# Scales of the feed-forward tiles on GpSimd instead of VectorE, the gate's Tanh over its input, a column of scales per tile, new call lists and banks

## The chip, the cores and the metric

The kernel runs on one core of one Trainium2 chip. Its five instruction queues are those of TensorE (PE), VectorE (DVE), ScalarE (ACT), GpSimd (POOL) and SyncE (SP); each works strictly in order and they meet only at semaphores. The metric is the device time of one execution in microseconds (us), median over several runs; less is better.

## The reference

One layer over x of shape (4, 256, 256): a two-way linear recurrence feeds a gated state-space block, and a second one feeds a quantised feed-forward block. Cut to what matters:

```python
# recurrence, used twice with other w and u (k = v = fside)
ek = exp(min(k, 30)); ekv = ek * v
nf, df = scan(a*decay + ekv), scan(b*decay + ek)        # forward over time, and the same backward
r = sigmoid(x) * (nf + nb - ekv + euk*v) / max(df + db - ek + euk, 1e-8) * (0.8 + 0.2*tf)
# attention
z, xc, B, C, dt = split(r @ in_proj_w); xc = silu(causal_conv1d(xc))
y = ssd_chunked(elu(C)+1, elu(B)+1, xc, exp(-dt*exp(A_log))) + D*xc
x = x + (rms_norm(y) * norm_scale * silu(z)) @ out_proj_w
# feed-forward, on h = second recurrence gated with x
def act_quant(x):  s = 127 / clip(max|x|, 1e-5);  return clip(round(x*s), -128, 127) / s
h = silu(act_quant(rms_norm(h)) @ weight_quant(w1).T + b1)
h = layer_norm(gelu(h)) * ln_g + ln_b
x = x + act_quant(rms_norm(h)) @ weight_quant(w2).T + b2
```

## The kernel before

The batch index b has four values. For each b the kernel does: the recurrences of both blocks at once on DVE (four forward scans, L1230; four backward, L1239; `add_own`, L1250; a reciprocal by one Newton step from a seed that ACT makes with Relu, Ln, Exp, `recip`; `ratio`; `gated`, L1277, which makes uT); the attention block on PE, ACT and DVE (`features`, `conv_in`, `gate_in`, DVE's `conv_taps` L1323, `conv_turns`, `running_sums`, `log_decays`, ACT's `decays` L844, DVE's `attend` L1347, `within`, `between`, `y_turns`, `project`); and the feed-forward block. That one works in eight tiles i of 128 rows, two for each b. `PARTS` numbers five parts p: for b = 0, 1, 2 both tiles together, and the last two tiles, 6 and 7, alone as p = 3 and 4.

A part's steps are `residual` (DVE L1375), `gate_h` (ACT), `ffn_in` (DVE), `square_h` (ACT), `norm_h` (POOL), `ffn_in_max` and `ffn_in_scale` (DVE, hm and its reciprocal hq), `quantise_h` (POOL L542), `q1_turns` (PE), `turned_q1` (ACT L888). A tile's steps are `ffn_diag` (POOL L482), `ffn_up` (PE; four matmuls of the activations with w1T and then four records of the bias row with the tile's diagonal, b1b and diag), `ffn_silu`, `ffn_gate` (tiles 4 to 7), `ffn_gelu`, `ffn_mean`, `ffn_var` (ACT L918), `ffn_dev` (POOL), `ffn_center` and `ffn_shift` (DVE L1435, L1443), `ffn_square` (ACT L930), `ffn_rms` (POOL), `ffn_max` and `ffn_scale` (DVE), `ffn_round` (POOL L576), a turn of the rounded tile (a DMA transpose for tiles 0 to 5, PE and ACT for 6 and 7), `ffn_down` (PE), `ffn_out` (DVE L1472) and `store` (SP).

Small scales go with it. `ffn_in_back` on DVE makes al1, which takes the product back to real units, two columns per part, and its reciprocal ral1, with which `ffn_diag` scales the identity, so that the bias is right before al1 is applied. `ffn_back` on DVE makes al2 for `ffn_out`. The scales of a part (hss, hmv, hr, hmx, hfl, hm, hq) live in tiles of two columns that the next part writes again, so `norm_h`, `ffn_in_max`, `ffn_in_scale` and `square_h` wait for the last readers of the part before. `gate_x` (ACT L752) writes Tanh of xcT into one buffer th, and so waits for `gated` of the b before.

The order of all this is written by hand at the end of each engine's block, as one list of calls; that list is the schedule. `HOME` gives every product its PSUM bank, and the bare `pe.wait_ge` lines between PE's calls wait until a bank's last reader is done. `warm(k)` issues eight matmuls that nobody reads. SP's list is the order of the loads, of `spread_sums` (six small DMAs that carry cum_s to cum_t, needed by `log_decays`), of the transposes `turn_q2` and of the stores. ACT's list also names its table loads.

Of the kernel before, what the change touches and what calls it, by code (L numbers as in the profile page):

```python
# [15 lines left out]
P = 128  # L16
# [14 lines left out]
    "warm": (4, 2, 1, 3, 5, 0, 4, 1, 2, 6),  # L31
    "cond_sum": 1,
    "weight_sums": 7,
    "features": (7, 1, 6, 5),
    "conv_in": ((3, 2), (6, 3), (4, 1), (6, 0)),
    "conv_turns": ((2, 3), (7, 2), (1, 0), (7, 6)),
    "gate_in": ((5, 1), (3, 5), (6, 4), (4, 5)),
    "r2_turns": (0, 4, 7, 7),
    "scores": (6, 0, 5, 4),
    "log_decays": (((0, 0), (5, 2)), ((6, 3), (5, 7)), ((6, 0), (0, 4)), ((7, 5), (2, 3))),  # L40
    "running_sums": (4, 1, 2, 5),
    "within": ((0, 2), (3, 5), (1, 4), (5, 6)),
    "between": (5, 2, 0, 2),
    "y_turns": ((5, 2), (1, 0), (2, 7), (2, 3)),
    "project": (1, 1, 0, 7, 6),
    "q1_turns": (0, 3, 3, 2, 2),
    "ffn_up": (2, 6, 2, 0, 4, 0, 6, 2),
    "weight_columns": 1,
    "ffn_turns": ((0, 0), (0, 0), (0, 0), (0, 0), (0, 0), (0, 0), (6, 7), (2, 3)),
    "ffn_down": (7, 3, 4, 5, 0, 1, 4, 5),  # L50
# [3 lines left out]
def build(nc, x, xT, kT, condT, wcol, prm, hprm, in_w, out_w, w1, w2, b1, ln_g, ln_b, b2, out):  # L54
# [23 lines left out]
    with ExitStack() as ctx:  # L78
# [15 lines left out]
        PARTS = [(b, 0, TT) for b in range(B - 1)] + [(B - 1, c, c + 1) for c in range(TT)]  # L94

# [66 lines left out]
        th = sb("th", [P, CT * T])  # L162
# [47 lines left out]
        ral1 = sb("ral1", [P, NT])  # L210
# [90 lines left out]
        def _(sp):  # L301
# [94 lines left out]
            store(4)
            store(5)
# [6 lines left out]
        def _(pool):  # L404
# [1666 lines left out]
```

## Time and profile before

| | us |
|---|---|
| median of 3 runs | 205.26 (204.13 to 205.44) |
| span of the profiled execution | 201.1 |
| TensorE busy in it | 159.6 |
| VectorE busy in it | 178.6 |
| ScalarE busy in it | 159.8 |
| GpSimd busy in it | 100.3 |

The span runs from the first to the last instruction of one execution; what the run's time has over it lies outside (before the first and behind the last instruction). Starts in the rows are microseconds from the span's start. A float32 matmul stands in the rows as two records of PE, so "x16" of float32 is eight matmuls, and the lengths given for single records overlap: a stretch is best read from start to start.

### The profile page before, as it was taken

To read this page: it belongs to the slowest core of one execution; us is meant where nothing else is said; L and a number is where in the kernel's file an instruction comes from. 1 tells how busy PE (TensorE), PEld (TensorE's weight loads), DVE (VectorE), ACT (ScalarE), POOL (GpSimd) and SP (SyncE) were. 2 spreads that over 40 slices of the span, in tenths; PEclk is the share of its full clock that TensorE was granted. 3 is DMA by queue.
4 is the path that set the end of the run, shared out by engine and by line. 5 is a ranking of instruction groups with operands and counts; after the bars stand their busy time and mean duration, and the time that the engine had idled before them with its cause. 6 is when DMAs were issued, how large, how long until landed. Compare 5 with 4: busy or idle time off the path is not lost.

```text
span 201.1 us, 3190 instructions
## 1 busy us (share of the span) xinstructions
PE 159.6 (79%) x903; PEld 117.4 (58%) x908; DVE 178.6 (89%) x320; ACT 159.8 (79%) x293; POOL 100.3 (50%) x172
## 2 busy tenths in 40 slices
PE   7800039459799999999999999999999999672844
PEld 5600038334589867698757488957668766350633
DVE  2899999999999999899999899979866769998991
ACT  5860599969699279998789999899999886877632
POOL 3609759000426523758700086467455287858570
PEclk9975557958999999999999999999999999999699
DMA  4999603200000000000000000000240000602312
GB/s 133 320 385 382 248 2 104 106 3 2 1 0 3 0 0 2 4 3 0 2 2 3 0 0 3 0 2 0 54 96 14 0 0 0 130 7 49 81 60 96
DMA packets 12304, 11.55 MB, mean 57 GB/s; under 512 B 7680, under 2 KB 10368, under 8 KB 12032
## 3 DMA queue, kind: packets, MB, share of 16 engines
q1 hardware_dynamic: 11856, 11.33, 18.1%
q8 instruction: 7, 0.11, 0.2%
q14 instruction: 9, 0.07, 0.1%
q10 hardware_dynamic: 432, 0.03, 0.1%
HBM read 8.69 MB, written 1.05 MB: 48 GB/s over the span
## 4 chain that ended last, share of the span: by engine, by line
PE 45%; DVE 14%; ACT 12%; issue 12%; POOL 8%; DMA 5%; SPq 3%; POOLq 1%; DVEq 0%; ACTq 0%
PE banks L1688 41%; DVE Ys L1239 5%; DMA wn<-wn 4%; PE banks L1685 3%; DVE Fs L1230 3%; DVE nd L1250 3%; SPq L355 2%; ACT Ys L744 1%; POOL qr L514 1%; ACT Ys L742 1%; POOL wn L576 1%; ACT dec L691 1%; ACT dec L844 1%; ACT D L724 1%; DMA cum_t<-cum_s 1%
## 5 line engine op out<-in xcount | busy, mean ns | idle before, releaser
L1688 PE MATMUL banks<-inw,uT 128*128 128x8 f32 (+1 forms) x64 | 21.7, 465 | 19.4 <-DVE uT L1277 19.4
L1688 PEld LDWEIGHTS banks<-inw,uT 128*128 128x128 f32 x64 | 10.9, 217 | 24.7 <-issue 24.5
L1230 DVE TENSOR_TENSOR_SCAN Fs<-D,E 128x514 f32<-128x514 f32 x16 | 23.0, 1460 | 0.5 <-POOL D L449 0.5
L1688 PE MATMUL banks<-uT,inw 128*128 128x256 f32 x80 | 20.3, 398 | 0.0
L1239 DVE TENSOR_TENSOR_SCAN Ys<-D,Fs 128x514 f32<-128x514 f32 x16 | 19.7, 1250 | 0.0
L1323 DVE SCALAR_TENSOR_TENSOR cv<-banks,cols,cv 128x255 f32<-128x255 f32 (+2 forms) x48 | 19.4, 472 | 0.1
L1688 PEld LDWEIGHTS banks<-uT,inw 128*128 128x128 f32 x80 | 15.2, 197 | 4.2 <-issue 2.1
L508 POOL TENSOR_TENSOR vs<-vv,grow 128x512 f32<-128x512 f32 x4 | 4.5, 1121 | 25.8 <-issue 20.3
L1688 PEld LDWEIGHTS banks<-vv,skips 128*128 128x128 f32 x128 | 15.2, 192 | 1.9 <-issue 1.8
L495 POOL TENSOR_TENSOR own<-own,vT 128x1024 f32<-128x1024 f32 x4 | 12.1, 3025 | 8.4 <-DVE own L1220 8.4
L1688 PE MATMUL banks<-vv,dec 128*128 128x64 f32 x128 | 15.6, 275 | 0.0
L1688 PE MATMUL banks<-vv,skips 128*128 128x64 f32 x128 | 15.3, 273 | 0.0
L1688 PE MATMUL banks<-b1b,diag 128*128 128x512 f32 x32 | 15.0, 592 | 0.0
L1688 PE MATMUL banks<-outw,yzT 128*128 128x256 f32 x64 | 15.0, 382 | 0.1
L1688 PEld LDWEIGHTS banks<-vv,dec 128*128 128x128 f32 x128 | 14.9, 192 | 0.0
L501 POOL TENSOR_TENSOR nd<-nd,Ys 128x512 f32<-128x512 f32 x4 | 5.2, 1301 | 17.5 <-DVE Ys L1261 17.5
L1688 PE MATMUL banks<-w2T,wn 128*128 128x256 f16 x64 | 9.0, 290 | 6.0 <-DMA wn<-wn 6.0
L1688 PE MATMUL banks<-starts 128*128 128x256 bf16 x80 | 12.1, 317 | 1.3 <-POOL starts L429 1.3
L1688 PEld LDWEIGHTS banks<-outw,yzT 128*128 128x128 f32 x64 | 11.8, 190 | 2.3 <-issue 0.5
L742 ACT ACTIVATE Ys<-nd 128x1024 f32<-128x1024 f32 (+1 forms) x5 | 4.4, 885 | 9.9 <-DVE nd L1250 9.9
L930 ACT ACTIVATE wn<-wn,grs 128x1024 f16<-128x1024 f32 x8 | 9.2, 1146 | 2.6 <-DVE wn L1443 1.5
L1347 DVE TENSOR_TENSOR dec<-dec,banks 128x1024 f32<-128x1024 f32 x8 | 9.7, 1210 | 1.7 <-ACT dec L844 1.7
(205 smaller groups left out, 469.4 us busy)
## 6 DMA issues: line engine op xcount, KB each, us to landing
wn<-in_w_dram SPq DMA_DIRECT2D x2, 1024.0 KB, 11.1
inw<-in_in_w_dram SPq DMA_DIRECT2D x1, 1160.0 KB, 10.8
vT<-in_kT_dram SPq DMA_DIRECT2D x4, 256.0 KB, 8.2
xcT<-in_xT_dram SPq DMA_DIRECT2D x4, 256.0 KB, 9.6
xn<-in_x_dram SPq DMA_DIRECT2D x4, 256.0 KB, 6.0
out_dram<-ot SPq DMA_DIRECT2D x8, 128.0 KB, 1.7
outw<-in_out_w_dram SPq DMA_DIRECT2D x1, 512.0 KB, 5.7
b1b<-in_b_dram SPq DMA_DIRECT2D x1, 512.0 KB, 8.6
```

The source lines that it names most:

```text
L495: pool.tensor_tensor(own[:, b % 2, :, 1, :], own_e(b), vT[:, b].unsqueeze(1).broadcast_to([P, 2, CT * T]), ALU.mult)\
L501: pool.tensor_tensor(nd[:, 1, 1], nd[:, 1, 1], rn[:, 1], ALU.mult).then_inc(rat2_ok, 1)
L508: pool.tensor_tensor(by_head(vs[:]), by_head(vv[:, b % 2, 0]), grow[:, 0, :].unsqueeze(2).broadcast_to([P, NH, HD]), ALU.mult).then_inc(vs ...
L742: act.activation(seed, den, ACT.Relu, bias=-DEN_FLOOR).then_inc(rl_ok, 1)
L930: act.activation(Q2[:, i % 2], Y[:, i % 2], ACT.Square, scale=grs[:, i:i + 1], accum_out=qss[:, i:i + 1])\
L1230: dve.tensor_tensor_scan(Fs[:, w, k], D[:, w, 0:CT * TS], E[:, b % 2, k].rearrange("p c t -> p (c t)"), 0.0, ALU.mult, ALU.add).then_inc(f ...
L1239: dve.tensor_tensor_scan(Ys[:, w, k][:, ::-1], D[:, w, 1:CT * TS + 1][:, ::-1], Fs[:, w, k][:, ::-1], 0.0, ALU.mult, ALU.add).then_inc(ys_ ...
L1250: last = dve.scalar_tensor_tensor(nd[:, :, w, s], y, gap[:, w, ct, b:b + 1], own[:, b % 2, w, :, s], ALU.mult, ALU.add)
L1323: dve.scalar_tensor_tensor(cv[:, ft, back:], at("conv_in", b, i)[:, j * T:(j + 1) * T - back], cols[:, w:w + 1], cv[:, ft, back:], ALU.mul ...
L1347: dve.tensor_tensor(dec[:, c], dec[:, c], at("scores", b)[:, c * P:(c + 1) * P].unsqueeze(1).broadcast_to([P, NH, P]), ALU.mult).then_inc( ...
L1685: return pe.transpose(dst, src, ident[0:n, 0:n])
L1688: return pe.matmul(dst, lhsT, rhs, start=start, stop=stop)
```

## The change

`ffn_in_back` and `ffn_back` are gone from DVE. POOL's `ffn_diag` makes al1 and a second column hsw (the root of the mean square over the weight scale), and the diagonal from hsw and hq; `ffn_round` makes al2 behind the rounding. The scales have one column per tile, and the waits for their last readers are gone. `gate_x` writes over xcT. Every call list is new, and so are the banks in `HOME` and the bare waits that go with them.

```diff
             def ffn_diag(i):
+                s = slice(i, i + 1)
                 pool.wait_ge(ident_ok, 2)
-                pool.wait_ge(al1_ok, 2 * part_of(i) + 2)
+                pool.wait_ge(hr_ok, part_of(i) + 1)
+                pool.wait_ge(hq_ok, part_of(i) + 1)
+                pool.wait_ge(wmean_ok, 3)
+                pool.tensor_scalar(al1[:, s], hm[:, s], hr[:, s], (wmean if i < FIRST_TANH else whalf)[:, 0:1], ALU.mult,
+                                   ALU.mult).then_inc(al1_ok, 1)
+                pool.tensor_scalar(hsw[:, s], hmv[:, s], hr[:, s], wrec[:, 0:1], ALU.mult, ALU.mult).then_inc(al1_ok, 1)
                 if i >= 2:
                     pool.wait_ge(h_ps, i - 1)
-                pool.tensor_scalar(diag[:, i % 2], ident[:], ral1[:, i:i + 1], 1.0 if i < FIRST_TANH else 0.5, ALU.mult, ALU.mult).then_inc(dg_ok, 1)
+                pool.wait_ge(al1_ok, 2 * i + 2)
+                pool.tensor_scalar(diag[:, i % 2], ident[:], hsw[:, s], hq[:, s], ALU.mult, ALU.mult).then_inc(dg_ok, 1)
...
                 pool.tensor_scalar(Q2[:, i % 2], Y[:, i % 2], qq[:, i:i + 1], ROUND16, ALU.mult, ALU.add)\
                     .then_inc(Q2_ok, 1)
+                s = slice(i, i + 1)
+                pool.wait_ge(qr_ok, 2 * (i + 1))
+                pool.tensor_scalar(al2[:, s], qm[:, s], gq[:, s], wmean[:, 1:2], ALU.mult, ALU.mult).then_inc(al2_ok, 1)
...
             def gate_x(b):
                 act.wait_ge(xT_in[b], 16)
-                if b >= 1:
-                    act.wait_ge(u_ok, b)
-                act.activation(th[:], xcT[:, b], ACT.Tanh, scale=0.5).then_inc(th_ok, 1)
+                act.activation(xcT[:, b], xcT[:, b], ACT.Tanh, scale=0.5).then_inc(th_ok, 1)
```

Of the lists, these parts matter most to the text below (the list after; "..." marks what is left out):

```text
SP    load_k(1) load_cond load_k(0) load_outw load_b1 load_xT(0) load_w1 load_xT(1) load_w2 ... load_inw ...
ACT   load_decw exp_w cond_tanh load_cols wkv_exp(0) wkv_exp(1) wkv_own(0) ...   (the first table load is no longer named)
PE    cond_sum warm(6) features(0) conv_in(0,1) conv_in(0,0) warm(8) ...          (before: 48 warm matmuls stood ahead of features(0))
DVE   ... ratio(0) forward(1,0,0) gated(0) recip(0,1,2) forward(1,0,1) forward(1,1,0) features(0) softplus_in(0)
      conv_taps(0,1) softplus_out(0) ... running_sums(0) wkv_min(2) conv_taps(0,0) recip(1,0,2) own_min(2) ratio(1) gated(1) forward(2,0,0) ...
DVE   ... recip(2,0,2) wkv_min(3) ratio(2) forward(3,0,0) gated(2) conv_taps(1,0) residual(0) ...
PE    ... project(0) log_decays(1,0,1) log_decays(1,1,0) features(2) gate_in(2,0) log_decays(1,1,1) conv_turns(1,0) conv_turns(1,1) ...
PE    ... within(3,0) q1_turns(2) r2_turns(3) between(3) ffn_up(4) y_turns(3,0) within(3,1) project(3) y_turns(3,1)
      weight_columns project(4) ffn_up(5) ffn_down(0) q1_turns(3) q1_turns(4) ffn_down(1) [wait Y_ok 5] ffn_up(6) ffn_up(7)
      [waits] ffn_down(2) ffn_down(3) ffn_down(4) ffn_down(5) ffn_turns(6,*) ffn_turns(7,*) ffn_down(6) ffn_down(7) [wait ot_ok 7] warm(0) warm(3)
ACT   ... turned_y(3,0) ffn_square(2) ffn_silu(4) ffn_square(3) square_y(3,1) ffn_gelu(4) turned_y(3,1) gate_h(3) weight_columns
      square_h(3) ffn_var(4) gate_h(4) square_h(4) ffn_silu(5) turned_q1(3) ffn_gelu(5) turned_q1(4) ffn_var(5) ffn_square(4)
      ffn_silu(6) ffn_square(5) ffn_gelu(6) ffn_silu(7) ffn_var(6) ffn_gelu(7) ffn_var(7) ffn_square(6) ffn_square(7) ...
DVE   ... ffn_shift(3) ffn_gate(4) ffn_scale(2) norm_gate(3,1) residual(3) ffn_max(3) ffn_mean(4) ffn_in(3) ffn_scale(3) residual(4)
      ffn_in_max(3) ffn_in(4) ffn_in_scale(3) ffn_in_max(4) ffn_center(4) ffn_in_scale(4) ffn_gate(5) ffn_shift(4) ...
```

Before, PE's list at this place was `within(3,0) between(3) q1_turns(2) within(3,1) y_turns(3,0) ffn_up(4) y_turns(3,1) project(3) ffn_up(5) project(4) q1_turns(3) ffn_down(0) ffn_down(1) [wait ot_ok 1] ffn_up(6) q1_turns(4) ffn_down(2) ffn_down(3) [wait ot_ok 2] ffn_up(7) ffn_down(4) warm(2) warm(7) ffn_down(5) ...`, with `weight_columns` far earlier and `r2_turns(3)` ahead of `within(3,0)`.

## Rows read from the trace of the kernel before

**Rows 1.** The page: busy tenths of each engine in 40 slices of the span
```profile
PE   7800039459799999999999999999999999672844
DVE  2899999999999999899999899979866769998991
ACT  5860599969699279998789999899999886877632
```

**Rows 2.** Windows: stretch, its length, busy us and instructions of each engine, PEclk, DMA
```profile
100.00:149.60 49.60, 49.10 (x258) 34.59 (x260) 44.60 (x78) 46.64 (x78) 21.20 (x38) 1.00 0.05 12
149.60:168.75 19.15, 19.10 (x115) 14.47 (x114) 14.01 (x29) 17.71 (x33) 10.86 (x30) 1.00 0.08 15
168.75:201.10 32.35, 18.65 (x124) 12.60 (x124) 26.39 (x49) 18.83 (x33) 20.60 (x47) 0.95 0.27 66
```

**Rows 3.** Groups by line, DVE: the scales that the change takes away
```profile
L1464 DVE TENSOR_SCALAR al<-qm,gq,wmean 128x1 f32<-128x1 f32 x8 | 2.0, 266 | 0.0
L1416 DVE TENSOR_SCALAR al<-hm,hr,whalf 128x1 f32<-128x1 f32 x4 | 1.0, 263 | 0.0
L1420 DVE RECIPROCAL ral<-al 128x2 f32<-128x2 f32 (+1 forms) x5 | 0.8, 165 | 0.2
```

**Rows 4.** Groups by line, POOL: its nearest operations to the added ones
```profile
L567 POOL TENSOR_SCALAR qfl<-qmv,qr,stdf 128x1 f32<-128x1 f32 x8 | 2.7, 334 | 0.0
L566 POOL TENSOR_SCALAR gq<-qr,grs 128x1 f32<-128x1 f32 x8 | 2.1, 264 | 0.8
L482 POOL TENSOR_SCALAR diag<-ident,ral 128x128 f32<-128x128 f32 x8 | 3.0, 371 | 8.0 <-issue 7.9
```

**Rows 5.** Timeline of the start: ACT's table load and Exp; then DVE's first scan
```profile
1.20 1.28 ACT L946 ACT_TABLE_LOAD   x1 [1.20 <-PEq L2061]
2.50 0.20 ACT L675 ACTIVATE ew<-decw 128x4 f32<-128x4 f32 x1
...
7.06 2.34 DVE L1230 TENSOR_TENSOR_SCAN Fs<-D,E 128x514 f32<-128x514 f32 x1 [0.53 <-POOL D L449]
```

**Rows 6.** Timeline: a scan beside a long product of POOL, and one alone
```profile
14.67 3.19 POOL L495 TENSOR_TENSOR own<-own,vT 128x1024 f32<-128x1024 f32 x1 [6.34 <-DVE own L1220]
15.64 3.30 DVE L1230 TENSOR_TENSOR_SCAN Fs<-D,E 128x514 f32<-128x514 f32 x1
54.03 1.22 DVE L1230 TENSOR_TENSOR_SCAN Fs<-D,E 128x514 f32<-128x514 f32 x1
```

**Rows 7.** Timeline: uT of b = 0, 1 and 2 on DVE, and the first cum_t on PE
```profile
26.84 1.56 DVE L1277 SCALAR_TENSOR_TENSOR uT<-th,nd 128x512 f32<-128x512 f32 x1
51.83 0.38 PE L1688 MATMUL banks<-cum_t,cum_s 99*128 99x512 bf16 x1 [1.38 <-DMA cum_t<-cum_s]
55.17 0.66 DVE L1277 SCALAR_TENSOR_TENSOR uT<-th,nd 128x512 f32<-128x512 f32 x1
82.99 0.68 DVE L1277 SCALAR_TENSOR_TENSOR uT<-th,nd 128x512 f32<-128x512 f32 x1
```

**Rows 8.** Timeline of the end: PE's anchor, project(4), quantise_h(4), ffn_up(7)'s bias, the last two roundings
```profile
151.53 1.95 PE L1688 MATMUL banks<-vv,dec 128*128 128x64 f32 x16
166.87 1.89 PE L1688 MATMUL banks<-outw,yzT 128*128 128x256 f32 x8
174.39 0.48 POOL L542 TENSOR_SCALAR h<-h,hq 128x256 f32<-128x256 f32 x1
180.35 1.88 PE L1688 MATMUL banks<-b1b,diag 128*128 128x512 f32 x4
...
193.30 2.33 POOL L576 TENSOR_SCALAR wn<-wn,qq 128x1024 f16<-128x1024 f32 x2
```

**Rows 9.** Windows of PE's clock: after the pause from 182.2, and the last stage
```profile
182.00:184.00 2.00, 0.34 (x2) 0.00 (x0) 1.45 (x5) 1.42 (x2) 1.82 (x4) 1.00 0.00 0
189.00:190.00 1.00, 1.00 (x6) 0.73 (x5) 0.94 (x1) 0.00 (x0) 0.85 (x3) 0.50 0.00 0
196.00:198.00 2.00, 2.00 (x23) 1.71 (x21) 0.48 (x1) 1.16 (x3) 0.44 (x1) 1.00 0.37 123
```

More of the change, by code:

```diff
@@ L30 @@
 HOME = {
[L31 to L50, printed above, removed]
+    "warm": (6, 7, 6, 0, 2, 1, 1, 6, 5, 7),
+    "cond_sum": 0,
+    "weight_sums": 1,
+    "features": (2, 0, 2, 3),
+    "conv_in": ((4, 3), (7, 3), (3, 7), (6, 7)),
+    "conv_turns": ((4, 4), (0, 6), (5, 3), (4, 4)),
+    "gate_in": ((0, 1), (0, 1), (3, 2), (5, 6)),
+    "r2_turns": (2, 4, 6, 4),
+    "scores": (5, 5, 0, 5),
+    "log_decays": (((3, 2), (6, 7)), ((4, 6), (4, 4)), ((7, 1), (5, 7)), ((1, 7), (6, 7))),
+    "running_sums": (3, 4, 1, 0),
+    "within": ((2, 6), (0, 1), (0, 7), (6, 6)),
+    "between": (1, 6, 3, 5),
+    "y_turns": ((0, 6), (4, 4), (1, 4), (7, 6)),
+    "project": (0, 2, 0, 7, 4),
+    "q1_turns": (2, 6, 7, 6, 5),
+    "ffn_up": (4, 1, 2, 0, 2, 0, 2, 5),
+    "weight_columns": 5,
+    "ffn_turns": (0, 0, 0, 0, 0, 0, (5, 2), (3, 2)),
+    "ffn_down": (7, 4, 0, 1, 7, 4, 6, 7),
 }
@@ L650, in _ @@
             ffn_rms(4)
+            residual_bias(3)
             ffn_rms(5)
@@ L1547, in _ @@
             conv_taps(1, 0)
-            recip(2, 0, 2)
-            ratio(2)
             residual(0)
-            wkv_min(3)
-            gated(2)
+            softplus_in(2)
+            attend(1, 0)
+            softplus_out(2)
+            forward(3, 0, 1)
+            forward(3, 1, 0)
             ffn_in(0)
-            attend(1, 0)
+            own_min(3)
             ffn_in_max(0)
-            forward(3, 0, 0)
-            forward(3, 0, 1)
+            features(2)
+            forward(3, 1, 1)
@@ L1558, in _ @@
+            attend(1, 1)
+            running_sums(2)
+            conv_taps(2, 1)
             y_scale(1)
[L1559 to L1560 removed]
+            clip_weights(0)
+            backward(3, 0, 0)
+            norm_gate(1, 0)
             ffn_in_scale(0)
[L1562 to L1569 removed]
@@ new lines, in _ @@
+            pe.wait_ge(r2_ok, 3)
+            conv_in(3, 0)
+            pe.wait_ge(ty_ok, 3)
+            features(3)
+            pe.wait_ge(att_ok, 6)
+            within(2, 0)
+            pe.wait_ge(cv0_ok, 7)
+            pe.wait_ge(tap_ok, 42)
+            within(2, 1)
+            pe.wait_ge(cv0_ok, 8)
+            pe.wait_ge(tap_ok, 48)
+            q1_turns(1)
+            pe.wait_ge(Y_ok, 1)
+            conv_turns(3, 0)
+            gate_in(3, 0)
+            pe.wait_ge(q1T_ok, 2)
+            gate_in(3, 1)
@@ L1992, in _ @@
-            r2_turns(3)
-            pe.wait_ge(dex_ok, 14)
+            pe.wait_ge(dex_ok, 15)
             within(3, 0)
-            pe.wait_ge(dex_ok, 15)
-            between(3)
             pe.wait_ge(dex_ok, 16)
             q1_turns(2)
+            pe.wait_ge(vv_ok, 8)
+            r2_turns(3)
+            pe.wait_ge(att_ok, 8)
+            between(3)
+            pe.wait_ge(Y_ok, 3)
+            ffn_up(4)
+            y_turns(3, 0)
             within(3, 1)
-            y_turns(3, 0)
-            ffn_up(4)
+            project(3)
```

785 lines of the change are left out of this document (365 added, 420 removed).

## The prediction

> **What bounds the kernel now.** I read the page's tenths first [rows 1]. DVE is full from the first scan (7 us) on, PE has almost nothing to do until about 28 us, and from about 60 us to 165 us PE is full too. The windows say it more exactly [rows 2]: from 100 to 149.6 us PE is busy 49.1 of 49.6 us, and to 168.75 us 19.1 of 19.15, while DVE has 5.0 and 5.1 us free there. ACT has 3.0 and 1.4 us free. Behind 168.75 us no engine is full (DVE 26.4 of 32.35 us, PE 18.7): there the last two tiles walk from engine to engine. So there are three stages. Up to uT of b = 1 (55.8 us [rows 7]) DVE's order sets the time. From there to about 165 us PE's queue does. The last 32 us are a chain of latencies, whose length the order on DVE, ACT and POOL decides. I take the stages apart in that order and ask of each what the new lists make of it, adding durations along the new lists.
>
> **The small scales.** DVE loses eight al2 of 0.266 us, eight al1 of 0.263 (two groups like the row) and five reciprocals of 0.165 [rows 3]: 2.1 + 2.1 + 0.8 = 5.0, by the rows' totals 4.7 us. Nearly all of it lies behind 90 us, where DVE had 5 us free in 50 anyway, so up to 168.75 us it is worth nothing; the cover is PE's full queue. POOL gains 24 operations. Each has three small operands, like qfl at 0.334 us, and the lower bound is gq with 0.264 [rows 4]. I take 0.33, as the operands are like qfl's, and 0.07 for each diagonal, which now multiplies by two columns: 24 x 0.33 + 8 x 0.07 = 8.5 us on an engine that has 38 of 68 us free between 100 and 168.75 us [rows 2]. Ahead of a diagonal al1 and hsw are 0.7 us, but PE asks for the diagonal only after q1_turns, ACT's copy and half of `ffn_up`, over 1 us later: nothing. The one place on the path is al2 of tile 6 between the last two roundings, 0.33 us.
>
> **Start, up to uT of b = 1.** Three things change. (a) The table load of 1.28 us is no longer named ahead of the first Exp [rows 5]. If it now runs behind the wait for decw it costs up to 1.28 us, if ahead of it nothing. Before, the load ran from 1.20 to 2.48 us and the Exp began at 2.50, so some of it stays covered: I take 0.5, bounds 0 and 1.28. The cond_sum no longer stands behind eight warm matmuls, but its load is now behind load_k(1): a wash. (b) `forward(1,0,0)` stands ahead of gated(0), and conv_taps(0,1) ahead of running_sums(0), while forward(2,0,0) now follows gated(1). Counting DVE's work between the first scan and gated(1), `forward(2,0,0)` goes out (-1.2), own_min(2) comes in (+0.6), and conv_taps(0,1) has to wait for PE and ACT at the half clock that follows 19 us of pause (about +1.3). (c) DVE's scans are held up by POOL's long products: the scan at 15.64 us took 3.30 us beside one and a scan alone 1.22, so 2.1 us were lost there [rows 6]. In the new order the first such product starts while five small operations stand between it and the next scan, so about 1 us less is lost. The sum is +0.5 - 1.2 + 0.6 + 1.3 - 1.0 = +0.2; I call it 0, with bounds -1.2 and +1.3. The first cum_t on PE (51.83 us [rows 7]) comes some 2 us later, but conv_turns(0,*) can run before it, and PE is free of both when uT of b = 1 comes. uT of b = 0 (done at 28.4 us [rows 7]) stays within 1 us.
>
> On (c) the Trainium skill (SBUF — State Buffer, Who interferes with whom) says that a DVE instruction with two SBUF inputs and a GpSimd instruction that reads SBUF exclude each other for a whole instruction, whichever starts first. The trace agrees with it: the scan of 3.30 us ended 1.1 us behind the product [rows 6]. By this rule the change's own 24 reads of SBUF on POOL work against it, which is a rival below.
>
> **Middle, from 55.8 us to PE's anchor.** As anchor I take the second half of within(3,0), which began at 151.53 us [rows 8]. PE is full, so the anchor moves by PE's work ahead of it and by waits. Out of the stretch go weight_columns (0.87 us) and r2_turns(3) (0.44): -1.3. In comes a wait. The new list has features(2) and gate_in(2,0) ahead of conv_turns(1,*), and by the order of its work PE is there at about 81 us, while uT of b = 2 was done at 83.7 before [rows 7], and in the new list conv_taps(1,0) (2.4 us) is behind it but forward(3,0,0) (1.2) ahead. I get a wait of 0 to 1.8 us there and take 0.7. Sum -0.6, bounds -1.3 and +0.5. From b = 2 on I find DVE several us ahead of PE at each meeting (it has shed 4.7 us, and center(2) and shift(2), 2.4 us, now follow attend(3,*)), so no further wait enters the sum.
>
> **The end.** Behind the anchor PE has in the new list the rest of within(3,0) 1.73, q1_turns(2) 0.44, r2_turns(3) 0.44, between(3) 0.87, ffn_up(4) 2.6, y_turns 0.44, within(3,1) 4.33, project(3) 1.73, y_turns 0.44, weight_columns 0.87 and project(4) 1.73 (start to start; the last ran from 166.87 to about 168.6 us [rows 8]). Together 15.6 us, so project(4) ends at 167.1 on before's clock: 1.5 us earlier, since ffn_up(5) is now behind it. From there to the end of quantise_h(4) before took 6.3 us (to 174.87 [rows 8]); in the new list ffn_gate(5) and ffn_out(0), 1.2 and 0.4 us, no longer stand in between: 3.1 us earlier by then. ffn_up(7) no longer waits for ffn_out(1) and two ffn_down; it follows ffn_up(6) and ends at 178.8 instead of about 182.1 (its bias began at 180.35 [rows 8]): 3.3 us earlier. Then part is given back. Tanh(7) on ACT stands behind Gelu(6), which waits for ffn_gate(6), which stands behind ffn_shift(5) on DVE; ffn_var(6) waits for the rounding of tile 4, and POOL has residual_bias(3) and two `ffn_rms` ahead of that. Adding along DVE's and ACT's lists, Tanh(7) ends 1.7 us earlier, and the last rounding, which ended at 195.6 [rows 8], at 193.5 with the 0.33 us of al2: 2.1 us earlier. Behind it turns, copies, two ffn_down, ffn_out and the store are as before. The two warm(0) and warm(3) at the very end take 16 x 0.11 = 1.7 us behind the last ffn_down, less than output and store take (2.7 us), so 0. The end is worth -2.1; the bounds are 0 (all given back) and -3.3 (nothing given back).
>
> **Sum.** 0 - 0.6 - 2.1 = -2.7, so 201.1 becomes 198.4 us. The median of the runs shown is 205.26, 4.2 us over the span, and I keep that: 202.6 us.
>
> **The rivals.**
> The clock (0.12): after ffn_up(7) PE pauses until tile 4 is turned, and warm(2) and warm(7), which stood ahead of ffn_down(5), are gone. The row from 189 to 190 us shows the half clock, 1.2 GHz, after the pause that began at 182.2, and 196 to 198 shows the full one [rows 9]. If the last stage ran at half, the last turns and two ffn_down of 0.98 us cost 2.4 us more: 205.0. Against it: ffn_down(4) and (5) run back to back, 3.9 us at half clock, just before.
> The slower one (0.2): PE's wait at features(2). Everything of b = 1 stands behind it in PE's queue. If two scans ahead of gated(2) are each held up 2.1 us by a product of POOL, as in rows 6, the wait is 1.8 + 4.2 = 6.0 us, and with a late start (+0.5) the sum is 0.5 - 1.3 + 6.0 - 2.1 = +3.1: 208.4. It makes the kernel slower by over 1% from a wait of about 5 us on. For it speaks that PE has no slack behind it, against it that DVE's list leads by more than one operation there.
> The end gives all back (0.18): if DVE and ACT, not PE's order, set the end (DVE 82% busy [rows 2]), only the middle's -0.6 is left: 204.7.
> POOL's small operations hold DVE up (0.05): of the 24, some 8 fall before uT of b = 3, 2.7 us; where DVE sets the pace that gives 205.3. Its rule stands above under (c). DVE's 5.0 free us up to the anchor speak against it.
> The likeliest has 0.45.
>
> **Numbers.** 1% is about what a measurement of this kernel can tell from no change. Faster by over 1% means below 203.2: the likeliest case, most of its range, and a little of the others: 0.48. Within 1%: the clock, the given-back end and POOL's case: 0.30. Slower: 0.22. With all bounds at their good end the sum is -1.2 - 1.3 - 3.3 = -5.8 (199.5), at their bad end 1.3 + 0.5 + 0 = +1.8 (207.1). The range is 199.0 to 207.2.
>
> **What would show it.** Right: uT of b = 1 within 1 us of 55.8; the second half of within(3,0) near 151; ffn_up(7) ended some 3 us earlier, and the last rounding only about 2. Wrong: PE pauses between 60 and 150 us, above all ahead of features(2); a first scan later than 8 us; PEclk 0.50 behind 190 us. The place I trust least is the middle, where a hundred meetings of queues stand on my reading of the lists.

## The result and the profile after

The changed kernel takes 223.06 us (median of 4, 222.5 to 224.1), the kernel before 204.69 beside it: ratio 1.0915, 95% interval 1.086 to 1.097. The profiled execution has a span of 220.3 us against 201.1. The forecast was 202.6. Several of the versions tried further down spread over 4 to 9 us from one execution to the next, so a median of four is rough there, and single executions are given where a number can't be understood without them.

The page's tenths of the changed kernel, and the granted clock of TensorE in the same 40 slices of 5.5 us:

```profile
PE   2100019799897699999978999999999999791738
DVE  2969997799999993899999959999637787888861
ACT  4179662999988436759528789999899997587621
PEclk9999999969999556999996799999999999998558
```

Against [rows 1], DVE is no longer full in the middle, ACT has holes at a third and half of the span, and PE dips twice, each time ahead of a stretch in which PEclk shows 5 to 7. The windows that answer to [rows 2] (stretch, length, busy us of PE, PEld, DVE, ACT, POOL, clock, DMA):

```profile
100.00:149.60 49.60, 47.74 (x271) 38.03 (x272) 46.00 (x75) 39.92 (x69) 20.52 (x33) 0.93 0.01 2
149.60:168.50 18.90, 18.47 (x88) 11.86 (x89) 12.14 (x25) 17.86 (x34) 13.01 (x29) 1.00 0.08 16
184.90:220.30 35.40, 23.04 (x132) 14.55 (x131) 25.47 (x43) 19.25 (x34) 23.93 (x58) 0.81 0.25 60
```

The same milestones in both profiled executions (ends in us unless marked; before from [rows 5], [rows 7], [rows 8] and, for uT of b = 3, the line below), with two experiments that the text comes back to (the changed kernel with k(1) third; the one with four places mended: k(1) third, cols early, la early, norm_gate ahead):

```profile
119.06 1.32 DVE L1277 SCALAR_TENSOR_TENSOR uT<-th,nd 128x512 f32<-128x512 f32 x1
```

| | before | after | late by | grew by | k(1) third | norm_gate ahead |
|---|---|---|---|---|---|---|
| first scan (start) | 7.1 | 8.1 | 1.0 | 1.0 | 7.0 | 7.2 |
| uT of b = 0 | 28.4 | 31.8 | 3.4 | 2.4 | 30.6 | 29.4 |
| uT of b = 1 | 55.8 | 59.5 | 3.7 | 0.3 | 58.6 | 56.6 |
| uT of b = 2 | 83.7 | 94.1 | 10.4 | 6.7 | 87.5 | 85.5 |
| uT of b = 3 | 120.4 | 134.7 | 14.3 | 3.9 | 124.8 | 124.7 |
| within(3,0), second half (start) | 151.5 | 168.5 | 17.0 | 2.7 | 158.1 | 157.9 |
| project(4) | 168.8 | 185.0 | 16.2 | -0.8 | 174.7 | 174.5 |
| last rounding | 195.6 | 213.9 | 18.3 | 2.1 | 203.9 | 203.8 |
| span | 201.1 | 220.3 | 19.2 | 0.9 | 211.6 | 211.5 |

So 3.7 us are lost at the start, 13.3 in the middle and 2.2 at the end. The middle as windows, from uT of b = 1 to the second half of within(3,0), before and after:

```profile
55.80:151.50 95.70, 95.12 (x544) 72.01 (x547) 89.34 (x161) 85.50 (x159) 45.94 (x69) 1.00 0.05 10
59.50:168.50 109.00, 103.50 (x540) 79.47 (x541) 93.85 (x154) 84.93 (x157) 50.25 (x76) 0.91 0.06 17
```

TensorE's account nearly closes it. It stands idle for 5.5 us instead of 0.6, and it is busy for 8.4 us longer although 1.3 us of its work, by the prediction's count, have left the stretch. A granted clock of 0.91 over 109 us is 9.8 us lost by an estimate that takes all its work to go with the clock. 4.9 + 9.8 - 1.3 is 13.4 us. The largest piece lies between uT of b = 1 and b = 2. The timeline there, PE first, then DVE, then POOL (start, us, engine, line, operation, and in brackets the idle time before it):

```profile
73.41 1.10 PE L1657 MATMUL banks<-tri,la 128*72 128x128 f32 x4 [3.22 <-DVE la L1317]
74.30 3.52 PE L1657 MATMUL banks<-vv,skips 128*128 128x64 f32 x16
77.61 3.62 PE L1657 MATMUL banks<-vv,dec 128*128 128x64 f32 x16
81.02 2.02 PE L1657 MATMUL banks<-yy,ident 128*128 128x512 f32 x2
...
70.53 2.25 DVE L1309 SCALAR_TENSOR_TENSOR dtp<-dtx,dtl 128x16 f32<-128x16 f32 x1
72.88 0.38 DVE L1317 SCALAR_TENSOR_TENSOR la<-dtp,expa 128x72 f32<-128x72 f32 x2
...
69.82 2.93 POOL L505 TENSOR_TENSOR own<-own,vT 128x1024 f32<-128x1024 f32 x1
```

dtp is an operation on 16 columns; the four of its kind take 0.17 us in the median. Here it starts 0.7 us behind POOL's own_times_v(2) and ends 0.03 us behind it: 2.25 us. la is late by 2.1 us, PE stands for 3.2, and when it starts again it is at half clock, 1.2 GHz, for 13 us, though its queue is full. The windows of one us each:

```profile
72.00:73.00 1.00, 0.00 (x0) 0.00 (x0) 0.90 (x2) 0.00 (x0) 0.75 (x1) 0.82 0.00 0
73.00:74.00 1.00, 0.59 (x3) 0.62 (x4) 0.97 (x4) 0.00 (x0) 0.00 (x0) 0.50 0.00 0
85.00:86.00 1.00, 1.00 (x4) 0.82 (x3) 0.00 (x0) 0.97 (x2) 1.00 (x3) 0.50 0.00 0
87.00:88.00 1.00, 1.00 (x4) 0.34 (x3) 1.00 (x1) 0.00 (x0) 0.00 (x0) 1.00 0.00 0
```

A dec group of 16 took 3.62 us here and 1.9 at full clock. square_y(0,1) on ACT waits 4.2 us for the end of within(0,1), which this group belongs to, recip_seed(2) stands behind that, DVE waits 2.4 us for the seed, and uT of b = 2 comes late. The same pattern comes again at 114.5 us: PE pauses 1.81 us ahead of scores(2), which waits for norm_gate(1,0) on DVE, and the clock is at half from 117 to 123.6. Ahead of norm_gate, DVE was held up beside POOL once more (1.43 us for a cast that takes 0.28 alone, and 1.72 us for clip_weights instead of 1.20):

```profile
107.31 1.97 POOL L477 TENSOR_SCALAR wn<-wn,wrec 128x2048 f32<-128x2048 f32 x1
107.99 1.43 DVE L1346 CAST cum_s<-crest 40x256 bf16<-40x256 f32 x1
115.52 0.66 DVE L1372 TENSOR_TENSOR yy<-banks,zs 128x512 f32<-128x512 f32 x1
116.28 0.94 PE L1657 MATMUL banks<-bcf 64*128 64x128 f32 x6 [1.81 <-issue]
```

### The profile page after: what moved, and what is told of

It reads as the page before. It is cut to its first block and busy times, and to the rows that moved or that the text cites. A ratio compares the mean times of both kernels' runs of the same rounds, so it can differ in the third digit from the quotient of the medians.

```text
span 220.3 us, 3180 instructions
## 1 busy us (share of the span) xinstructions
PE 169.7 (77%) x903; PEld 126.4 (57%) x908; DVE 182.3 (83%) x299; ACT 160.5 (73%) x293; POOL 111.5 (51%) x196
## 5 line engine op out<-in xcount | busy, mean ns | idle before, releaser
L1657 PE MATMUL banks<-inw,uT 128*128 128x8 f32 (+1 forms) x64 | 20.1, 441 | 25.7 <-DVE uT L1283 25.7
L1657 PE MATMUL banks<-uT,inw 128*128 128x256 f32 x80 | 23.3, 446 | 0.0
L1657 PEld LDWEIGHTS banks<-uT,inw 128*128 128x128 f32 x80 | 17.6, 227 | 4.9 <-issue 2.2
L1657 PEld LDWEIGHTS banks<-vv,skips 128*128 128x128 f32 x128 | 16.9, 210 | 0.7 <-issue 0.5
L1657 PE MATMUL banks<-vv,dec 128*128 128x64 f32 x128 | 17.3, 293 | 0.0
L1657 PEld LDWEIGHTS banks<-vv,dec 128*128 128x128 f32 x128 | 16.6, 210 | 0.0
L498 POOL TENSOR_TENSOR E<-E,vT 128x512 f32<-128x512 f32 x4 | 5.7, 1418 | 17.6 <-DVE E L1222 17.6
L1256 DVE SCALAR_TENSOR_TENSOR nd<-Ys,gap,own 128x512 f32<-128x512 f32 x16 | 13.8, 913 | 0.0
L522 POOL TENSOR_SCALAR ymv<-yss 128x1 f32<-128x1 f32 x8 | 2.4, 306 | 21.9 <-ACT yzT L868 21.5
L1425 DVE SCALAR_TENSOR_TENSOR banks<-banks,nmu,xcT 128x1024 f32<-128x1024 f32 x8 | 10.3, 1287 | 1.6 <-issue 1.6
```

Of the source, the lines that this page charges most:

```text
L498: pool.tensor_tensor(E[:, b % 2, 1, :, 0:T], E[:, b % 2, 0, :, 0:T], vT[:, b].rearrange("p (c t) -> p c t", c=CT), ALU.mult).then_inc(ev_o ...
L522: pool.tensor_scalar(mv, src, scale, eps, ALU.mult, ALU.add).then_inc(mid, 1)
L1256: last = dve.scalar_tensor_tensor(nd[:, :, w, s], y, gap[:, w, ct, b:b + 1], own[:, b % 2, w, :, s], ALU.mult, ALU.add)
L1425: dve.scalar_tensor_tensor(ffn_mid(i), ffn_mid(i), nmu[:, i:i + 1], lngb, ALU.add, ALU.mult)\
L1657: return pe.matmul(dst, lhsT, rhs, start=start, stop=stop)
```

## The experiments

The theory that I set out with: the named edit is nearly free, and start, pauses and end of the new order cost the time. "Before" below is always the kernel before, run on the same chip with the kernels compared.

**The edit alone.** The kernel before with al1, diag's factor and al2 on POOL, a column per tile, and the calls ffn_in_back and ffn_back gone:

```text
+ pool.tensor_scalar(al1[:, s], hm[:, s], hr[:, s], ...)   in ffn_diag, with hsw and diag
+ pool.tensor_scalar(al2[:, s], qm[:, s], gq[:, s], ...)   in ffn_round
- ffn_in_back(0..4), ffn_back(0..7)                        in DVE's list
```

> The kernel before with one part of the change alone: al1, the factor of diag and al2 are computed by GpSimd, with a column of scales per tile; its own call lists, banks and Tanh stay. Theory A (the loss of 18 us lies in the new order, the named edit is nearly free): within 1% of the kernel before, 203 to 206.5 us. Rival B (GpSimd's eight and a half us of additional small operations hold up its queue or VectorE): slower by 2 to 4%, 209 to 213 us, and the anchor vv,dec of within(3, 0) more than 3 us later than 151.5.

Measured 208.20 against 205.12 us, ratio 1.014 (1.008 to 1.020): neither. It costs about 3 us (2.8 by the ratio), and most of it not in the middle (the anchor at 152.2, 0.7 late) but behind it. POOL's queue behind ffn_round(2), and DVE behind it:

```profile
170.96 0.38 POOL L588 TENSOR_SCALAR al<-qm,gq,wmean 128x1 f32<-128x1 f32 x1
171.43 1.12 POOL L584 TENSOR_SCALAR wn<-wn,qq 128x1024 f16<-128x1024 f32 x1
172.65 0.33 POOL L588 TENSOR_SCALAR al<-qm,gq,wmean 128x1 f32<-128x1 f32 x1
172.97 0.33 POOL L487 TENSOR_SCALAR al<-hm,hr,whalf 128x1 f32<-128x1 f32 x1
173.28 0.34 POOL L489 TENSOR_SCALAR hsw<-hmv,hr,wrec 128x1 f32<-128x1 f32 x1
...
175.25 0.26 POOL L540 TENSOR_SCALAR hfl<-hmv,hr 128x1 f32<-128x1 f32 x1
...
175.62 0.21 DVE L1408 TENSOR_SCALAR hm<-hmx,hfl 128x1 f32<-128x1 f32 x1 [1.44 <-POOL hfl L540]
```

hfl of part 4 was at 172.89 before, 2.4 us earlier; 0.7 of that is the late anchor. Four small operations more stand ahead of it now, and a diagonal that takes 0.45 us instead of 0.37. DVE waits 1.44 us, and the roundings of tiles 4 and 5 start 2.3 us later.

**The same, with POOL's queue mended.** norm_h(4) directly behind ffn_round(3), and al2 in calls of its own behind what DVE waits for:

```text
  ffn_round(2) ffn_round(3)
+ norm_h(4)
  ffn_diag(6) ffn_dev(4) quantise_h(4) residual_bias(3) ffn_diag(7) ffn_dev(5)
+ ffn_back(2) ffn_back(3)
```

> The kernel before with the scales on GpSimd as in the run of the scales alone, but with GpSimd's queue mended at its crowded place: norm_h(4) directly behind ffn_round(3), and al2 of tiles 2 to 7 in calls of its own behind the work that VectorE waits for. Theory A (what the scales cost is the 2.3 us by which hfl of part 4 comes late): hfl of part 4 within 0.5 us of 173.2, time 203 to 205.5 us. Rival B (each small operation on GpSimd costs the end, wherever it stands): 206.5 to 208.5 us as with the scales alone.

205.08 (10 executions) against 205.33, ratio 1.003 (0.998 to 1.009): no difference. hm of part 4 came at 175.0, not at 173.4, but the anchor was 1.6 us late in this execution too, so that behind the anchor it stands where it did. So the cost was the place, not the number of operations, and no gain from DVE's 4.7 us of relief can be seen. One control is missing: norm_h(4) was moved ahead of a diagonal as well, which the kernel before with nothing else changed was not given.

**Both edits in the old order.** The functions of the changed kernel, Tanh over its input too, in the lists and banks of before:

```text
  lists and HOME as before; load_lng, load_lnb behind spread_sums(0); make_tri ahead of make_late
```

> Both edits of the code (scales on GpSimd, the gate's Tanh over its input) in the call lists and banks of the kernel before; only the loads of ln_g and ln_b stand behind spread_sums(0), and make_tri ahead of make_late. Theory A (the edits are worth the 1.4% that the scales alone cost, all else of the 9% is the new order): 206.5 to 209.5 us. Rival B (the Tanh over its input, in new order or old, costs several us more): above 211 us. Rival C (the Tanh without the wait for the tile th gives something back): 204 to 206 us.

208.19 against 205.33, ratio 1.017 (1.010 to 1.025), as theory A says, and 208.20 with the scales alone: no price of the Tanh can be seen. The other 15 us are the order and the banks.

**The scales given back, in the new order.**

```text
+ ffn_in_back(p) behind ffn_in_scale(p), ffn_back(i) ahead of ffn_out(i), in DVE's list of the changed kernel
```

> The changed kernel with the scales given back to VectorE (al1, its reciprocal and al2 behind the calls that they follow, GpSimd's diag with one factor as before); its own order, banks and Tanh stay. Theory A (GpSimd's queue at the end is what the edit costs: in the kernel before with the edit alone hfl of part 4 came 2.3 us later and the time rose by 2.8 us): 2 to 4 us below 223.1, 219 to 221.5 us, with quantise_h(4) 1.5 to 2.5 us earlier than 189.9. Rival B (the new order has taken the queue's load into account, so the edit is worth its VectorE time here): the same or up to 2 us slower, 222.5 to 225 us.

222.64 us (218.0, 221.2, 224.1 and 224.7). In the profiled execution (224.1), in which dtp was held up as in the changed kernel's, quantise_h(4) came 0.7 us later than there instead of earlier, and project(4) 1.0 us later: rival B. So in like executions the new lists do hide the edit; the executions at 218.0 and 221.2, which have no profile, leave the median too rough to say it to a microsecond.

**The first loads, both ways.**

```text
changed kernel:  load_cond load_k(0) load_k(1) load_outw ...
kernel before:   load_k(1) load_cond load_k(0) load_xT(0) load_outw ...
```

> The changed kernel with one load moved: SyncE issues k(1) as its third load, behind cond and k(0), instead of first. Theory A (256 KB ahead of the small loads makes decw, condc and cols land late, which moves the first scan by 1.0 us and the first own by more): first scan back at 7.0 to 7.3 instead of 8.06, uT of b0 1 to 3 us earlier than 31.8, time 1 to 3 us below 223.1. Rival B (the shift of the start is made good later, at a wait for something else): first scan earlier but the time within 0.8 us of 223.1. Rival C (the late landings have another cause): first scan still at 8.

> The kernel before with one load moved: SyncE issues k(1) ahead of cond and k(0). Theory A (256 KB ahead of the small loads cost the start its microsecond or more): first scan at 8.0 to 8.3 instead of 7.06, uT of b0 1 to 2.5 us later than 28.4, time 206 to 207.5 us. Rival B (made good later): first scan late, time within 0.7 us of the kernel before. Rival C (the order of the loads has nothing to do with it): first scan at 7.1.

In the kernel before k(1) ahead costs 1.4 us (204.83 against 203.47, 11 and 13 executions; ratio 1.0065, 1.004 to 1.009), with the first scan at 7.82. The landing of decw went from 1.6 to 2.8 us after its issue, and uT of b = 0 came 0.8 us later. In the changed kernel k(1) third brings the first scan back to 7.0 and uT of b = 0 to 30.6. Both are as theory A says; the time, 218.72, is lower than its range, but in single executions it is 213.8, 217.6, 219.9 and 221.6. The first was the profiled one, and its trace suggests where the spread comes from.

**cols early as well.**

```text
  load_decw()
+ load_cols()
  exp_w() cond_tanh()
- load_cols()
```

> The changed kernel with k(1) as SyncE's third load, and besides the load of cols issued right behind that of decw on ScalarE's queue instead of behind two activations. Theory A (cols, which the first own waits for, landed at 7.9 us against 4.6 and this is what is left of the late start): uT of b0 at 28.5 to 29.5 instead of 30.6 with k(1) third alone, and the best executions at 211 to 213 us, 1 to 2 us below the 213.8 of k(1) third alone. Rival B (the rest of the late start is the order of VectorE's list): uT of b0 at 30.3 to 30.8, the best executions at 213.5 to 214.5 us.

cols landed 2.0 us after issue instead of 7.9 in the changed kernel, but uT of b = 0 stayed at 30.5 in this execution, as rival B says. Three later versions with the same edits of the start had it at 29.3, 29.4 and 29.9, though. What set it here is on ScalarE: the Tanh of xT(0) and then of xT(1), which stand ahead of the first seed in the new list, waited 4.45 and 2.59 us for their loads, and DVE waited 1.69 us for the seed:

```profile
11.98 0.63 ACT L760 ACTIVATE xcT<-xcT 128x512 f32<-128x512 f32 x1 [4.45 <-DMA xcT<-in_xT_dram]
15.20 0.63 ACT L760 ACTIVATE xcT<-xcT 128x512 f32<-128x512 f32 x1 [2.59 <-DMA xcT<-in_xT_dram]
24.52 1.52 DVE L1264 SCALAR_TENSOR_TENSOR tn<-nd,Ys 128x512 f32<-128x512 f32 x1 [1.69 <-ACT Ys L756]
```

In the version with norm_gate ahead the two Tanh began 1.3 us earlier, DVE waited 0.27 us, and uT of b = 0 came 1.1 us earlier. The executions took 211.7, 219.4, 219.7 and 221.1; the best is where theory A put it, the profiled one is the last. DVE and POOL in it further on, then the same in the profiled execution of the kernel with only k(1) third, which took 213.8:

```profile
69.19 2.25 DVE L1309 SCALAR_TENSOR_TENSOR dtp<-dtx,dtl 128x16 f32<-128x16 f32 x1
68.48 2.93 POOL L505 TENSOR_TENSOR own<-own,vT 128x1024 f32<-128x1024 f32 x1
```

```profile
69.57 0.15 DVE L1309 SCALAR_TENSOR_TENSOR dtp<-dtx,dtl 128x16 f32<-128x16 f32 x1
69.97 2.44 POOL L505 TENSOR_TENSOR own<-own,vT 128x1024 f32<-128x1024 f32 x1
```

Here dtp came 0.40 us ahead of POOL's product and took 0.15 us; there it came 0.71 behind and took 2.25. PE paused 3.21 us at running_sums(1) in the one (half clock from 71 to 85) and 0.32 in the other (full clock from 59 to 89). uT of b = 2 was done at 92.7 and at 87.5. All five profiled executions with dtp at 2.25 us took 221 to 224 us. That the executions without a profile fall apart for the same reason is likely but not shown.

**la earlier.**

```text
+ softplus_out(1)
  forward(2, 1, 0) forward(2, 1, 1) backward(2, 1, 0)
- softplus_out(1)
```

> The changed kernel with one call moved: VectorE's softplus_out(1) (dtp and la, 0.4 us) runs ahead of forward(2, 1, 0) instead of behind backward(2, 1, 0). Theory A (the pause of TensorE at running_sums(1), behind a dtp held up for 2.25 us beside GpSimd's product, halves the clock for 13 us and this makes uT of b2 late): no pause above 1 us near 70, the granted clock at 1.00 from 73 to 86, uT of b2 5 to 8 us earlier than 94.1, and the time 5 to 9 us below 223.1, 214 to 218 us. Rival B (VectorE's own load sets uT of b2, the clock is a bystander): less than 2 us gained, 221 to 223.5 us. Rival C (another pause a little later halves the clock instead): clock 0.50 for several us between 70 and 100 still, 220 to 223 us.

217.29 us (214.7 to 219.8), ratio to before 1.050 instead of 1.092: 5.8 us for the place of 0.4 us of work, as theory A says. No pause above 0.6 us was left near 70, and the clock was at full from 60 to 91. uT of b = 2 came at 89.7, 4.4 us earlier and not 5 to 8. The pauses at features(2) (1.77 us, half clock from 91 to 95) and at scores(2) (1.76 us, 115 to 122) remained.

**The pause filled, in the changed kernel.**

```text
+ warm(10) four times ahead of running_sums(1), in its bank
```

> The changed kernel with TensorE's pause kept but filled: four blocks of eight bf16 multiplications into a bank that nobody reads, ahead of running_sums(1), each about 0.9 us. The late la stays as it is, only the idleness of TensorE goes. Theory A (the idleness costs the clock, and the clock the time): granted clock 1.00 from 73 to 86, within(0, 1) at half its length (5.5 us less), uT of b2 4 to 7 us earlier, 215 to 219 us. Rival B (the late la itself is what costs): clock 1.00 but time within 1.5 us of 223.1.

220.56 us, which settles nothing: in the profiled execution the clock had already fallen at 56 us (half until 67), dtp took 0.15 us, and the four blocks ran where there was no pause to fill.

**The pause made in the kernel before, and then filled.** The clean form of the same question.

```text
- softplus_out(1)
  add_own(2, 0) add_own(2, 1) norm_gate(0, 1)
+ softplus_out(1)
```

> The kernel before with one call moved the other way: VectorE's softplus_out(1) behind norm_gate(0, 1), so that la comes 4 us later and TensorE stands at running_sums(1) for about 3 us, as in the changed kernel. Theory A (a pause of TensorE of 3 us at this place puts its clock at half for 7 to 13 us): granted clock 0.50 for at least 6 us between 72 and 90, uT of b2 3 to 8 us later than 83.7, time 207 to 213 us. Rival B (the clock does not fall behind a single pause of 3 us): clock 1.00, uT of b2 within 2 us, time 204 to 206.5 us.

> The kernel before with la 4 us late as in the run that made the pause, and three blocks of eight bf16 multiplications into a free bank in front of running_sums(1), so that la is as late and TensorE not idle. Theory A (idleness costs the clock, and the clock most of the time): granted clock 1.00 from 70 to 90, uT of b2 1.5 to 3.5 us later than 83.7 instead of 5.3, time 205 to 208 us against 209.4 to 214.3 of the pause unfilled. Rival B (the lateness of la costs as much by itself): 209 to 213 us with the clock at 1.00.

Unfilled 212.44 (209.4 to 214.3; ratio 1.027, 1.014 to 1.040), filled 206.34 (206.0 to 208.5, 10 executions; ratio 1.009, 1.005 to 1.013), before 205.3 and 205.4. PE unfilled, and a window behind the pause (the clock is the third number from the end):

```profile
76.19 0.86 PE L1688 MATMUL banks<-tri,la 128*72 128x128 f32 x4 [2.52 <-DVE la L1311]
```

```profile
78.00:82.00 4.00, 4.00 (x10) 2.35 (x10) 3.27 (x11) 2.35 (x4) 1.97 (x1) 0.50 0.01 2
```

and filled:

```profile
72.32 2.78 PE L1688 MATMUL banks<-starts 128*128 128x256 bf16 x24
75.13 0.63 PE L1688 MATMUL banks<-tri,la 128*72 128x128 f32 x4
```

```profile
76.00:84.00 8.00, 7.92 (x43) 5.97 (x42) 6.94 (x16) 6.76 (x11) 1.98 (x1) 1.00 0.01 2
```

la is late in both (done at 76.0 and 75.0; before 71.7, and this unfilled execution was 1.2 us late already when PE reached running_sums(1)). With PE idle for 2.5 us its clock is at half until 84 and uT of b = 2 comes at 89.0; with PE busy on nothing the clock stays and uT comes at 86.4 (before: 83.7). So of the 7.1 us of the pause about 6 are the idleness and 1 the lateness: theory A in both, and the loss of the changed kernel in a kernel that never had it.

**The second pause.** First ScalarE's 5.1 us at the weights, then VectorE's order:

```text
ACT, first run:   square_y(1, 1) turned_y(1, 0) weight_done(0)       (weight_done(0) stood ahead of both)
DVE, third run:   norm_gate(1, 0) clip_weights(0) backward(3, 0, 0)  (norm_gate(1, 0) stood last)
```

> The changed kernel with ScalarE's weight_done(0), which stands 5.1 us for wclip, moved behind turned_y(1, 0), so that square_y(1, 1) is not behind it. Theory A (this wait delays yss, TensorE pauses 1.8 us ahead of scores(2) and its clock is at half from 117 to 123.6): no pause there, clock 1.00 from 116 to 124, uT of b3 3 to 5 us earlier than 134.7, time 2.5 to 5 us below 223.1. Rival B (uT of b3 hangs on VectorE, held up beside GpSimd): uT of b3 within 1.5 us of 134.7, time within 1.5 us.

> The changed kernel with k(1) third, cols loaded early, softplus_out(1) ahead of forward(2, 1, 0) and weight_done(0) behind turned_y(1, 0). Theory A (start 1.5 to 2, first pause 6 to 7, second 3 to 4 us, and the prices add): median 209 to 212.5 us, no half clock between 60 and 185 but for short stretches, uT of b2 at 86.5 to 88, of b3 at 124 to 126. Rival B (the pauses move to another place as soon as one is mended): median 213 to 218 us.

> The changed kernel with k(1) third, cols loaded early, softplus_out(1) ahead of forward(2, 1, 0), and norm_gate(1, 0) ahead of clip_weights(0) on VectorE. Theory A (scores(2) waits for its bank until norm_gate(1, 0) has read it, which stands 2 us behind clip_weights(0), and the clock falls behind that pause): no pause above 0.5 us ahead of scores(2), granted clock 1.00 from 108 to 120, uT of b3 at 123 to 125.5 instead of 127.5, time 211 to 213.5 us against 215.9. Rival B (the pause comes from elsewhere on ScalarE or moves by a call): still half clock for 7 us between 105 and 125, 214.5 to 217 us.

weight_done(0) behind gave 223.23 us, and the pause was there at the same place (116.43, 1.82 us): not the cause. With start and la mended too 215.88 us (215.5 to 217.1), in rival B's range: the first pause was gone, the second not (109.05, 1.78 us; half clock from 111 to 118; uT of b = 3 at 127.5). With norm_gate(1, 0) ahead, which reads the bank that scores(2) writes, no pause above 0.25 us was left between 86 and 120, and uT of b = 3 came at 124.7; the time is 214.21 (212.2 to 216.2), 1.7 us less, with overlapping ranges, and just outside theory A's. The wait at features(2), which the version without this move had too (1.76 us, half clock from 87 to 91), was still there, and this time 7 us of half clock followed it:

```profile
85.65 1.36 PE L1657 MATMUL banks<-inw,uT 128*128 128x8 f32 x8 [1.77 <-DVE uT L1283]
```

```profile
86.00:93.00 7.00, 7.00 (x18) 3.92 (x18) 6.03 (x14) 3.73 (x8) 1.34 (x1) 0.51 0.00 0
```

This execution alone does not test the move, since DVE was not held up in it. With norm_gate(1, 0) in its old place ten executions were profiled. In nine an operation on cum_s took 1.2 to 2.2 us beside POOL's product with wrec (0.28 or 0.41 alone), clip_weights took 1.7 to 2.0 us instead of 1.2, and PE paused 1.76 to 1.82 us ahead of scores(2). In the tenth, with k(1) third, neither was held up and there was no pause. With norm_gate ahead and al2 behind the pairs (below) the operation on cum_s did take 1.99 us, and PE did not pause at scores(2), so the move works there. But it paused 2.21 us a call later, at conv_turns(2,0), with half clock from 111 to 115, and uT of b = 3 came at 127.3: as rival B says, the pause moved.

**The end.** Warm multiplications as the kernel before has them ahead of ffn_down(5), then all three mended places, then al2 behind each pair of roundings:

```text
  ffn_down(4) [wait ot_ok 2]
+ warm(10) warm(10)
  ffn_down(5)
```

> The changed kernel with two more blocks of eight bf16 multiplications on TensorE between ffn_down(4) and ffn_down(5), into the bank that ffn_down(5) writes next, as the kernel before has them there. Theory A (without them TensorE is idle from 206 to 212 us and its clock is at half until 215.5, where the last down-projections run): granted clock back at 1.00 by 210, ffn_turns and ffn_down(6) at half their length, 1 to 2.5 us below 223.1. Rival B (the end hangs on GpSimd's and VectorE's chain, TensorE's clock is a bystander): within 0.8 us of 223.1 though the clock is back.

> The changed kernel with three places mended together: k(1) as third load, softplus_out(1) ahead of forward(2, 1, 0), two blocks of multiplications ahead of ffn_down(5). Theory A (start, pause at running_sums(1) and end each have their own price, and the prices add): 223.1 less 1.5 (start) less 5.5 (pause) less 1.5 (end), 213 to 216 us, with uT of b2 at 87 to 88.5. Rival B (the three are one, whatever keeps TensorE from pausing does it all): 216 to 219 us, as with one of them alone.

> As the run with norm_gate(1, 0) ahead, and GpSimd's al2 in calls of its own behind each pair of roundings instead of between them. Theory A (0.33 us between the last two roundings is on the path, and 0.3 to 0.7 us more at the pair before): 0.3 to 1.2 us below that run. Rival B (al2 is covered): the same within 0.3 us.

The blocks gave 221.42 us (219.5 to 224.5) against 223.06, and the clock still fell, from 202 to 209 and again from 212 to 220: so neither theory was put to the test. The three together gave 213.94 (213.3 to 219.1), in theory A's range, though the clock fell at the end here too. al2 behind the pairs gave 215.64 with one execution at 211.4 and three at 215.5 to 217.4, beside 214.21: the 0.33 us don't show in this spread.

## Why the prediction was wrong

**"From there to about 165 us PE's queue does" (set the time): right,** and it is why the rest went wrong. A full queue has no slack for a pause, and I gave the clock a rival only for the end.

**Middle, "no further wait enters the sum": this step failed.** The sum had -0.6 with bounds -1.3 and +0.5; measured is +13.3. I counted DVE's lead in us of work and took it that an operation of 0.15 us can't be late. It was, by 2.1 us, because it began behind POOL's product of 2.93 us. The pause that it made was then multiplied by the clock (6.7 us at uT of b = 2). The 3.9 us up to uT of b = 3 have the same form but not the same origin: cum_s and clip_weights held up beside POOL, a pause of 1.8 us, and the clock again. That second pause was there in four profiled executions in which dtp was not held up. In the sum the two idle stretches and the half clock behind them are nearly all of the 13.3 us, as the windows above show. The wait at features(2) that I took at 0.7, and at 6.0 in the slower rival, did not happen: PE came there late itself. With the pauses ahead of it mended it is 1.8 us, the upper end I gave. A further 2.7 us went between uT of b = 3 and the anchor, at full clock, PE busy 33.4 of 33.8 us: within(2,0), 3.5 us of PE, ran ahead of that uT before (at 116.4) and behind it after (at 140.1). That is work that changed sides of the milestone, not a wait.

**The slower rival** had the right direction and place in kind (a wait of PE in the middle, made by a hold-up beside POOL) and a price without the clock. It asked for 5 us of wait to decide; the runs show that 2.5 are enough, as they bring 5.3 us of delay at uT of b = 2.

**The hold-up:** the Trainium skill (SBUF — State Buffer, Who interferes with whom) says that a DVE instruction with two SBUF inputs and a GpSimd instruction that reads SBUF exclude each other for the whole instruction, whichever comes first. Both profiled cases agree: 2.25 us when dtp was second by 0.7, 0.15 us when it was first by 0.4. I applied it to long scans and to POOL's new small operations, whose own lock is 0.33 us; it matters most for the shortest DVE operation that someone waits for.

**Start, "0, bounds -1.2 and +1.3": outside, +3.7.** The table load cost nothing (it ran at 1.2 us, ahead of the wait). k(1) ahead of the small loads, which I called a wash by looking at cond_sum alone, moved decw and the first scan by 1.0 us. uT of b = 0 within 1 us failed by 3.4. In the changed kernel DVE waited 1.79 us for the first own, which stands behind the landing of cols. Where cols landed earlier, the wait for the seed took its place, and 1.2 us came and went between executions with the landing of xT(0) and xT(1), which this seed now stands behind on ScalarE. What remains beyond that (29.3 against 28.4 at best) was not tried by itself. The 1.0 us of (c) did not come, at least: no scan was held up beside POOL's first own product, but make_decay was, to 2.64 us from 0.59, which is as much as the scan had lost before.

**The small scales, "up to 168.75 us worth nothing": right; "the one place on the path is al2 of tile 6": wrong.** POOL's operations took what I gave them (medians: al 0.34, hsw 0.34, diag 0.45). In the old order they cost 2.8 us, most of it through POOL's queue ahead of hfl of part 4, a reader that I didn't name; in the new order they cost nothing that can be measured. DVE's relief bought nothing that can be seen in either. POOL had 36.7 us free between 100 and 168.75 us, not 38 [rows 2]; nothing hangs on it.

**The end, -2.1: measured +2.2.** project(4) came 0.8 us earlier behind the anchor (I had 1.5), ffn_up(7) earlier still: from the anchor to its end 30.7 before and 28.5 now. But the last rounding came 2.1 us later behind project(4), and the stretch behind it took 0.9 us more, with the half clock from 202 to 216 (0.81 on average behind 184.9) over the last turns and part of ffn_down. My clock rival had this, and it is a small piece of the loss. Where DVE and ACT lost the lead that PE gave them was not settled. With four places mended, project(4) to the end takes 37.0 us (before 32.3, after 35.3): 29.3 up to the last rounding (before 26.8) and 7.7 behind it (before 5.5), at half clock until 209.

**What stays open.** The best of the mended versions, 213.9 and 214.2 us, are still 9 to 10 us behind the kernel before beside them (203.5 and 205.1). In the profile of the last they lie at 0.8 up to uT of b = 1, 4.9 from there to project(4) (the wait at features(2) with its 7 us of half clock, and the place of within(2,0)) and 4.7 at the end. No version was faster than the kernel before.

## What to carry to other kernels

Where TensorE is full, look for the instruction that it waits for next and ask what that one could be second to: a 16-column DVE operation behind a 2.9 us GpSimd product made its reader 2.1 us late by itself and cost 6 to 7 us with the clock that fell behind the pause. Move such an operation ahead of its neighbours, or give TensorE something to multiply in the gap. And work moved to an idle engine is free only if nobody waits for what is queued behind it: the same 24 operations cost 2.8 us in one order of POOL's queue and nothing that could be measured in another.

## What the runs showed of the hardware

- After a pause of 2.5 to 3.2 us in a full queue, the clock was at half for 8 us (76 to 84) and 13 us (73 to 86), with PE busy throughout; after pauses of 1.8 us for 7 us (117 to 123.6, 111 to 118, 86 to 93; in the second a pause of 0.9 us lay 2 us behind the first). In other executions a pause of 1.8 us at features(2) was followed by 4 us (89 to 93).
- With 24 bf16 multiplications in a gap of 2.8 us, the clock stayed at full.
- With one 256 KB load issued ahead, a 2 KB load on another queue landed 2.5 us after its issue instead of 1.6 (2.8 in the kernel before). For the 14 KB of cols the effect is not separated: 5.1 instead of 4.6 us in the kernel before; in the changed one 7.9 with k(1) first, 6.1 and 7.6 with it third, and 2.0 when cols itself was issued 3 us earlier.
- A DVE operation on 16 columns took 0.15 us when it came 0.4 us ahead of GpSimd's product and 2.25 us when it came 0.7 behind. uT of b = 2 lay over 5 us apart in these two executions, which are of two versions that differ in the load of cols alone. Executions of one version lay up to 9 us apart (211.7 and 221.1).
